# Attention one of a language-model tower: the normalisation of a half in four parts, its projections two slots later

## The reference, cut to what matters

```python
h = W.T[tokens]                                   # 8 x 1024 tokens, 256 wide
h = h + attention_one(layernorm(h))               # 16 heads of 16
h = h + experts(layernorm(h))
h = h + attention_two(layernorm(h))
h = h + ffn(layernorm(h))

def attention_one(x):
    q, k, v = split(einsum('bhce,ef->bhcf', heads(x), Wqkv) + bqkv)
    att = einsum('bhqe,bhke->bhqk', q, k) / 4
    att = softmax(att * tril(ones, k=-1))         # masked scores are 0, not -inf
    return merge(einsum('bhqk,bhke->bhqe', att, v)) @ Wr + br
```

## Time and profile before

| what | value |
|---|---|
| median of 3 runs | 2991.42 us (2987.37 to 2992.92) |
| profiled execution, its own time | 2990.82 us |
| profiled span, first to last instruction | 2989.1 us |
| busy, share of the span | PE 91%, DVE 70%, POOL 59%, ACT 53% |
| mean granted TensorE clock | 0.938 |

### The profile page before, as it was taken

One profiled execution on the slowest core, in us unless ns is written; L12 is line 12 of the kernel. 1 busy time (PEld: TensorE's weight loads), 2 busy tenths in 40 slices (PEclk: granted clock), 3 DMA queues, 4 the chain that ended last, 5 costly groups with the idle time before them and its releaser, 6 DMA issues. The chain is left out here.

```text
span 2989.1 us, 60158 instructions
## 1 busy us (share of the span) xinstructions
PE 2718.0 (91%) x14648; PEld 1584.0 (53%) x14742; DVE 2097.0 (70%) x5794; ACT 1589.8 (53%) x3630; POOL 1750.2 (59%) x3265
## 2 busy tenths in 40 slices
PE   3788899898898898898868999999999979999999
PEld 1344444444454444444445666666666646766666
DVE  4466766666676676676546999999999865555554
ACT  1455666665666665666522555555555534444444
POOL 3874444444444444444343777777777757777775
PEclk8788999999999999999968999999999979999999
DMA  2343233233223233223130000000000000000000
GB/s 41 86 79 44 26 38 42 24 41 43 30 34 42 25 39 43 35 29 42 22 137 1 1 1 0 0 0 0 0 0 0 1 2 17 16 14 16 16 16 18
DMA packets 60127, 79.13 MB, mean 26 GB/s; under 512 B 20364, under 2 KB 32408, under 8 KB 59416
## 3 DMA queue, kind: packets, MB, share of 16 engines
q1 hardware_dynamic: 55240, 67.74, 16.2%
q0 software_dynamic: 3072, 8.39, 0.9%
q10 hardware_dynamic: 1744, 2.16, 0.2%
HBM read 18.98 MB, written 8.39 MB: 9 GB/s over the span
## 5 line engine op out<-in xcount | busy, mean ns | idle before, releaser
L463 ACT ACTIVATE probs<-scoresT 128x512 f32<-128x512 f32 (+3 forms) x1536 | 695.3, 491 | 497.8 <-PE scoresT L601 489.6
L551 DVE TENSOR_REDUCE cand<-ring 128x4 f32<-128x512 f32 x1152 | 729.2, 681 | 189.9 <-PE ring L653 169.0
L384 POOL TENSOR_SCALAR_AFFINE_SELECT probs<-probs 128x128 f32<-128x128 f32 x1024 | 293.3, 295 | 523.1 <-ACT probs L463 518.6
L601 PE MATMUL scoresT<-stage 98*128 98x512 bf16 (+3 forms) x1536 | 489.3, 360 | 75.5 <-ACT probs L463 63.6
L653 PE MATMUL ring<-stage 96*128 96x512 bf16 (+2 forms) x1792 | 421.2, 310 | 28.3 <-DMA stage<-parts 14.3
L615 PE MATMUL pv<-probs,Vg 128*32 128x512 f32 (+3 forms) x3072 | 314.5, 513 | 3.5 <-POOL probs L384 3.4
L601 PEld LDWEIGHTS scoresT<-stage 98*128 98x128 bf16 x1536 | 146.2, 99 | 280.1 <-ACT probs L463 221.4
L653 PEld LDWEIGHTS ring<-stage 96*128 96x128 bf16 x1792 | 161.1, 99 | 223.6 <-DVE cand L551 96.8
L1131 ACT ACTIVATE hT<-mmT,w_be,w_g 128x128 f32<-128x128 f32 x512 | 185.3, 468 | 156.2 <-PE mmT L1061 156.2
L1070 PE MATMUL mm<-w_W,x2T 128*128 128x512 f32 x512 | 257.6, 626 | 0.0
L1050 PE MATMUL mm<-w_W,hT 128*128 128x256 f32 x1024 | 257.0, 394 | 0.0
(11 more groups left out here) (252 smaller groups left out, 5369.1 us busy)
## 6 DMA issues: line engine op xcount, KB each, us to landing
stage<-parts SPq DMA_DIRECT2D x256, 96.0 KB, 3.1
stage<-parts SPq DMA_DIRECT2D x256, 64.0 KB, 3.2
stage<-parts SPq DMA_DIRECT2D x256, 32.0 KB, 2.9
out<-result SPq DMA_DIRECT2D x64, 128.0 KB, 1.7
stage<-ct SPq DMA_DIRECT2D x128, 4.0 KB
w_W<-in_W SPq DMA_DIRECT2D x4, 512.0 KB
h<-in_WT,tok POOLq DMA_INDIRECT x64
stage<-in_tok_ SPq DMA_DIRECT2D x1, 1024.0 KB, 4.8
```

The source lines that it names most:

```text
L384: nc.gpsimd.affine_select(out=d, in_=d, compare_op=ALU.is_gt, fill=0.0, base=0, pattern=[[1, P]], channel_multiplier=-1).then_inc(mask_ok, 1)
L463: nc.scalar.activation(probs[:, n % 8, lo:hi], scoresT[u % SCORE_BANKS][:, lo % 512:(hi - 1) % 512 + 1], ACT.Exp, scale=SOFT).then_inc(exp ...
L551: ins = nc.vector.tensor_reduce(c, src[:].rearrange("p (t a b) -> p t a b", t=c.shape[1], b=P), AX.X, ALU.max)
L601: nc.tensor.matmul(scoresT[u % SCORE_BANKS][:, lo % 512:(hi - 1) % 512 + 1], Ks[0:ROWS, gi, hh, P * kt:P * kt + P], Qs[0:ROWS, gi, hh, lo: ...
```

## The change

In window 0 the eight tiles are normalised in four parts of two. The statistics stand in slots 1, 2, 3 and 4 instead of all in slot 1, each part with its own wait between bn_stats and bn_aggr. POOL's step is an event of its own, `LN_POWER`, in slot 4 instead of slot 3, and waits for all four parts. DVE's normalisation stands in slots 4, 5, 6 and 7 instead of slot 3. `XT` goes from slot 6 to 8, the four `QK` from slots 8, 10, 12, 14 to 10, 12, 14, 16, and the `MID` that follows each from 10 to 16 to 12 to 18. `V`, `SUF`, `PT`, `MX` and all of window 1 keep their slots. Ahead of the first half the parts stand behind each other.

```diff
--- before.py
+++ after.py
@@ -47,6 +47,8 @@
 MAX_BANKS = len(MAX_PLAN)
 FUTURE = -2.0 ** 126
 SCORE_BANKS, RING_BANKS = 2, 4
+LN_PARTS = 4
+LN_TILES = TPB // LN_PARTS
 
 
 def score_units(kt, hh):
@@ -78,7 +80,7 @@
 
 
 AT = {
-    0: {"LN_STATS": 1, "LN_NORM": 3, "XT": 6, "PV_COPY": 0, "TMP": 0, "PT": 5, "OT": 21, "WR": 22, "RSUM": 5, "SUF": 9, "QK": 8, "QK_STEP": 2, "MID_LAG": 2, "V": 12, "VG": 0, "LOAD": 11, "MX": 6, "MX_END": 29, "MX_CURVE": 1.2},
+    0: {"LN_STATS": 1, "LN_NORM": 4, "XT": 8, "PV_COPY": 0, "TMP": 0, "PT": 5, "OT": 21, "WR": 22, "RSUM": 5, "SUF": 9, "QK": 10, "QK_STEP": 2, "MID_LAG": 2, "V": 12, "VG": 0, "LOAD": 11, "MX": 6, "MX_END": 29, "MX_CURVE": 1.2},
     1: {"PV_COPY": 0, "TMP": 0, "PT": 2, "WR": 1, "V": 8, "VG": 6, "LOAD": 6, "MX": 3, "MX_END": 28, "MX_CURVE": 1.2},
     "V_IN": 0, "WR_IN": 1,
 }
@@ -96,8 +98,11 @@
         others.setdefault(min(pos, 31), []).extend(events)
 
     if prologue:
-        at(pos_of["LN_STATS"], ("LN_STATS",))
-        at(pos_of["LN_NORM"], ("LN_NORM",))
+        for n in range(LN_PARTS):
+            at(pos_of["LN_STATS"] + (n if scores else 0), ("LN_STATS", n))
+        at(pos_of["LN_NORM"], ("LN_POWER",))
+        for n in range(LN_PARTS):
+            at(pos_of["LN_NORM"] + (n if scores else 0), ("LN_NORM", n))
         at(pos_of["XT"], ("R", "XT", "act", 0), ("R", "XT", "act", 1))
     if tail:
         at(pos_of["PV_COPY"], ("PV", -1, 7), ("PV_COPY", -1))
@@ -385,8 +390,8 @@
                                                     pattern=[[1, P]], channel_multiplier=-1).then_inc(mask_ok, 1)
                             if section == "first" and gi * 32 + n < TILES - TPB:
                                 gather(TPB + gi * 32 + n, gat1)
-                        elif kind == "LN_NORM":
-                            wait_apart(pool, (mv_ok, hb + 2))
+                        elif kind == "LN_POWER":
+                            wait_apart(pool, (mv_ok, LN_PARTS * (hb + 2)))
                             nc.gpsimd.tensor_scalar(rstd[:], mv[:, :, 1], EPS, None, ALU.add).then_inc(rs_c, 1)
                             pool.wait_ge(rs_c, hb + 2)
                             nc.gpsimd.tensor_tensor(rstd[:], rstd[:], minus_half[:], ALU.pow).then_inc(rstd_ok, 1)
@@ -517,16 +522,17 @@
                                 dve.wait_ge(gat0, 16 * TPB)
                             elif section == "loop":
                                 dve.wait_ge(gat1, 16 * (TILES - TPB))
-                            for t in range(TPB):
+                            part = range(LN_TILES * e[2], LN_TILES * e[2] + LN_TILES)
+                            for t in part:
                                 ins = nc.vector.bn_stats(st[:, t, :], h[:, TPB * (hn // 2) + t, :])
                             ins.then_inc(stats_c, 1)
-                            wait_apart(dve, (stats_c, hn + 1))
-                            for t in range(TPB):
+                            wait_apart(dve, (stats_c, LN_PARTS * hn + e[2] + 1))
+                            for t in part:
                                 ins = nc.vector.bn_aggr(mv[:, t, :], st[:, t, :])
                             ins.then_inc(mv_ok, 1)
                         elif kind == "LN_NORM":
                             dve.wait_ge(rstd_ok, hn + 1)
-                            for t in range(TPB):
+                            for t in range(LN_TILES * e[2], LN_TILES * e[2] + LN_TILES):
                                 nc.vector.tensor_scalar(xn[:, t, :], h[:, TPB * (hn // 2) + t, bass.ds(P * (hn % 2), P)],
                                                         mv[:, t, 0:1], rstd[:, t:t + 1], ALU.subtract, ALU.mult).then_inc(xn_ok, 1)
                         elif kind == "VG":
```

## The result

| | median, us | runs |
|---|---|---|
| before | 2992.17 (2987.37 to 2993.29) | 4 |
| changed | 3021.72 (3018.68 to 3024.07) | 4 |

The ratio is 1.0101, with a 95% interval from 1.0084 to 1.0119: the change costs 29.5 us. I had forecast the direction and 3007 us, a loss of 15.7; the time lies just outside the range, which ended at 3020.

The account below looks back on a forecast made before the run. Window 0 goes by ACT in slots 0 to 5, PE in 5 to 15, ACT in 16 to 19. 0.38 us times 15 = 5.7, plus 10 for the clock, makes 15.7: 3007 us, range 2983 to 3020.

Parts of the forecast that it names:

- Fourth projection from slot 14 to 16: Window 0: two evictions ahead of exp 17 cost 1.14 us; slot 19's score matmul starts 3.22 us behind slot 16's.
- The net of 0.28: Fourth projection's move in window 0: evictions cost 1.14 us, PE gains 0.86, so 0.28 us lost a half.
- The power one slot later: Window 0: DVE normalises 1.1 us later, the parts give that back; 0.1 us a half, bounds 0 and 1.1.
- the transposes: Window 0, two slots later on PE: as much PE work lies at the low clock as before, so 0.
- The first projection's wait for the load DMAs: Window 0: ACT's 0.95 us wait goes, but PE was busy throughout, so its removal gives nothing.
- Ahead of the first half: Statistics in parts, where nothing covers the waits between bn_stats and bn_aggr: 0.5 us, once.
- The clock: Start of window 1: long low stretches in 5 of 15 halves instead of 1; 4 more times 2.5 = 10 us.
- B: Loss without the clock: the long low stretch in window 1 stays as rare as before; 2997 us, chance 17%.
- C: Fourth projection's evictions mostly hidden, but halves pay the gain back to the clock's rise; 2987 to 2991 us, chance 18%.
- D: PE's 0.86 us in window 0 is kept because the evictions find idle time of ACT; 2980 us, chance 14%.
- E: DVE late too in window 0: 1.1 us a half instead of 0.1, 15 us on top of 3007; 3022, chance 3%.
- F: A further low stretch from PE's idle time ahead of slot 19, 2.0 us in 15 halves; 3037 us, chance 3%.

Follow-up runs that it names:

- filled kernels: Kernel before and changed kernel, each with PE matmuls of constants where PE waits (slots 1 to 3, window ends): 2979.06 and 2984.24 us.
- filled kernel before: Kernel before plus unused PE matmuls of constants, five in slots 1 to 3 and eight at each window's end: 2979.06 us, ratio 0.9962.

## Why the prediction was right and wrong

**Fourth projection from slot 14 to 16: right.** 1.14 us for the two evictions were 1.15, slot 19 was said to come at 3.22 and comes at 3.23, behind ACT's exp 17, and the projections alone bring all of the loss. The place was shown twice over: evictions ahead of exp 17 make the scores late, and behind it they make the ring late. The net of 0.28 is another matter: with the projections moved alone it is 0.14 at the upper clock and 0.65 in the one like pair of windows with the low stretch, because what stands in slots 8 and 9 waits for ACT differently.

**The power one slot later, 0.1, and the transposes, 0: right where the clock is as before, too small elsewhere.** No run takes the two apart. In the half with the clock as before they are 0.13 together (slot 6 is 0.88 shorter, and slot 8 1.01 longer beside the projection's 0.86), so the whole direct loss is 0.46, where I had 0.38. Where the low stretch begins earlier the same comparison gives more: the window 0 from 1099.87 us takes 51.03 against 50.15 (from 635.08 us before), 0.88 more. At the upper clock it is 0.58, of which the parts with the later power and the transposes one slot later cost 0.29 by themselves. The forecast looked at DVE's evictions, which do come as early as before, but not at who wants them earlier: the maxima have moved up to behind slot 6. While the clock is low there, PE's own work covers that; where it is high, PE waits 1.37 us. The transposes now run at the upper clock (1.04 us for 1.72) and what took their place runs at the lower, as forecast.

**The first projection's wait for the load DMAs: right in the kernel before.** It was hidden there. In the filled one it costs 0.44 us a half.

**Ahead of the first half.** The 0.5 us that the forecast allowed there is missing from its sum. The first score matmul stands at 80.44 us instead of 80.09, 0.35 later.

**The clock, four more long stretches at 2.5: this is the step that failed.** That a small loss grows through the clock is shown: without low stretches 8.1 of 27.3 us are left, and a wait of 0.1 us a half brings 7 us. Its size was wrong in two ways. The long stretches came in nine windows 1 of fourteen, not five of fifteen: I had let a half behind a long one stand so far off that the next would come after three, but up to three follow each other (windows 1 from 331.9, 423.4 and 515.24 us) before a short one comes. And the price: I had taken 2.0 in window 1 and 0.5 behind it, but the low stretch then also reaches over the end of window 1 into the window 0 behind it (462.72 to 476.35), which takes 51.27 instead of 50.48, 0.8 more. The 27.3 us are made up so: 14 x 0.46 = 6.4, the direct loss at the price of the half with the clock as before; another 14.4 - 6.4 = 8.0 in the windows 0, of which eleven take over 51.0; and 12.9 in the windows 1, where seven more are long. The forecast had 5.7 direct and 10 for all the rest, which is 20.9: this is the term that put the time outside the range.

**Rivals.** B (no clock) is out by the filled kernels. C and D are out by slot 19. E was right in kind (the later power shows where the clock is high or the parts are missing) and far below its price of 1.1 a half; that the measured time is E's 3022 is chance: E added 15 us of a late DVE, and what was missing lay in the clock. F was near to what happened: not a new low stretch ahead of slot 19, but longer ones at both window starts.

What stays open: why one, two or three long stretches come in a row and then leave one window 1 out. And the part of the program outside the fourteen halves differs by up to 6 us between profiled executions although its code is alike (1741.2 us before, 1746.9 in the filled kernel before), which blurs the medians by as much. It has low stretches of its own, and no run here looks at them.

## What to carry to other kernels

Before work is moved to a later slot, take every queue that it passes: here the matmul left a stretch that goes by PE, and its two evictions landed in front of an exp for which PE waits. A ring of four banks adds a second date to every eviction: four uses later the bank is wanted, so an eviction that gets out of one engine's way can get into another's.

In a loop whose PE clock falls and rises once or twice a turn, a small loss can cost more than its own length, as it did here. Look at the granted clock of each turn first, and where the clock falls ahead of work that goes by PE, try to fill the idle time ahead of the fall. Here 21 matmuls a half that nobody reads, put into waits, made the kernel 0.4% faster and the halves alike, so that a change of 0.1 us in one shows. But compare with care: holding the clock up also changes who waits for whom, and here it uncovered a wait of 0.44 us for the load DMAs that cost nothing before.

## What was not expected of the hardware

A wait of 0.10 us a half, 1.4 us in fourteen halves, made these halves 6.9 us longer and moved the median by 14 us. Eight matmuls of constants in the idle time at the end of each window and five in slots 1 to 3 kept the granted clock at 1.00 from the third half to the last filled one, where the earlier trace rows have 0.90 to 0.94. With the clock constant the windows of a kind had the same length from the third half on: 49.24 to 49.30 and 38.56 to 38.59 us.
